# Block steps of a four-layer sequence kernel: the gated squares in quarters, their halves added on GpSimd, one matmul a group

## The reference, cut to what matters

```python
zxbcdt = rmsnorm(x, norm_w) @ Win                  # 64 -> z 128, x 128, B 16, C 16, dt 8
xBC = silu(causal_conv(zxbcdt[..., 128:288], Wconv, bconv))
dt = softplus(zxbcdt[..., -8:] + dt_bias); A = -exp(A_log)
y = ssd(xh, dt, A, B, C) + rev(ssd(rev(xh), rev(dt), A, rev(B), rev(C)))
y = (y + D * xh) * silu(z)                         # 128 inner channels, the "gated" y
y = y * rsqrt(mean(y * y, -1) + 1e-6) * gn_w       # the mean over the 128 channels of a token
x = x + y @ Wout
```

## Time and profile before

| what | value |
|---|---|
| median of three runs | 2499.17 us |
| span of the profiled execution, first to last instruction | 2496.4 us |
| PE busy | 1980.1 us, 79% |
| DVE busy | 1670.7 us, 67% |
| ACT busy | 1666.6 us, 67% |
| POOL busy | 1090.7 us, 44% |
| mean granted TensorE clock | 0.891 |

### The profile page before, as it was taken

The page is one execution under the profiler, slowest core; times in us unless marked ns, Lnnn a source line. Parts: engine busy times, 40 slices in busy tenths (PEclk is TensorE's granted clock), DMA queues, the critical chain, the costliest instruction groups (busy, mean ns, idle before and its releaser), DMA issues.

```text
span 2496.4 us, 58563 instructions
## 1 busy us (share of the span) xinstructions
PE 1980.1 (79%) x24262; PEld 1001.1 (40%) x24262; DVE 1670.7 (67%) x2423; ACT 1666.6 (67%) x2731; POOL 1090.7 (44%) x858
## 2 busy tenths in 40 slices
PE   4367677776777679979979979967997997996996
PEld 3122222222222235535525535534553552553553
DVE  3488888888888766556656656656655765665663
ACT  1276677676676657757857857866775775785784
POOL 0044444444444525516606625623551660662563
PEclk6578888888988889989989989988988998998997
DMA  4000000000000021022012111102102201211111
GB/s 159 0 0 1 1 0 0 1 1 0 1 1 0 0 65 38 18 65 49 19 56 47 30 55 39 39 18 62 41 14 66 49 18 56 47 30 42 40 39 35
DMA packets 95513, 77.46 MB, mean 31 GB/s; under 512 B 65936, under 2 KB 74128, under 8 KB 94736
## 3 DMA queue, kind: packets, MB, share of 16 engines
q1 hardware_dynamic: 91984, 73.32, 11.7%
q10 hardware_dynamic: 3264, 0.39, 0.1%
HBM read 27.02 MB, written 11.53 MB: 15 GB/s over the span
## 4 chain that ended last, share of the span: by engine, by line
PE 55%; DVE 20%; ACT 15%; issue 6%; POOL 2%; DMA 1%; ACTq 0%; POOLq 0%; SPq 0%; DVEq 0%
PE bank L593 10%; PE bank L662 7%; PE bank L625 6%; PE bank L674 6%; PE bank L606 5%; PE bank L682 5%; DVE Z L1271 4%; PE bank L521 3%; ACT bank L935 3%; PE bank L577 2%; ACT Z L827 2%; DVE XP L1337 2%; ACT SS L832 2%; DVE bank L1263 2%; POOL Y L986 2%
## 5 line engine op out<-in xcount | busy, mean ns | idle before, releaser
L986 POOL TENSOR_TENSOR Y<-Z 128x512 f32<-128x512 f32 x256 | 330.6, 1292 | 496.9 <-DVE Z L1271 320.4
L1018 POOL TENSOR_TENSOR SQ<-SQ,folded_weights 128x512 f32<-128x512 f32 x192 | 243.8, 1272 | 676.0 <-DVE SQ L1448 675.9
L1271 DVE TENSOR_TENSOR_SCAN Z<-SS,bank 128x512 f32<-128x512 f32 x256 | 309.9, 1211 | 0.5
L521 PE MATMUL bank<-Y,constants 128*128 128x512 f32 x512 | 298.0, 668 | 7.7 <-DVE bank L1279 7.6
L1024 POOL TENSOR_TENSOR SQ<-O,SQ 128x512 f32<-128x512 f32 x208 | 264.8, 1274 | 64.9 <-ACT O L931 36.5
L593 PE MATMUL bank<-folded_weights,work 128*64 128x128 f32 x4096 | 287.2, 285 | 0.0
L625 PE MATMUL bank<-SS,work 32*128 32x512 bf16 x1024 | 209.7, 389 | 63.0 <-ACT bank L935 45.0
L662 PE MATMUL bank<-SQ,work 128*32 128x64 f32 x8192 | 259.1, 227 | 0.6
L593 PEld LDWEIGHTS bank<-folded_weights,work 128*64 128x64 f32 x4096 | 225.9, 140 | 79.0 <-issue 79.0
L509 PE MATMUL bank<-work,Z 96*128 96x512 bf16 x256 | 113.8, 445 | 175.1 <-DVE Z L1271 175.0
L1390 DVE SCALAR_TENSOR_TENSOR work<-SQ,bank 64x512 f32<-64x512 f32 x256 | 175.5, 685 | 108.7 <-ACT SQ L903 106.6
(11 more groups left out here) (264 smaller groups left out, 3757.5 us busy)
## 6 DMA issues: line engine op xcount, KB each, us to landing
work<-XP SPq DMA_DIRECT2D x256, 134.0 KB, 2.4
decays_kept<-extra SPq DMA_DIRECT2D x24, 384.0 KB, 2.3
SS<-decays_kept SPq DMA_DIRECT2D x256, 24.0 KB
block_weights<-callw SPq DMA_DIRECT2D x8, 735.0 KB, 4.3
work<-decays_kept SPq DMA_DIRECT2D x240, 24.0 KB
Z<-state_sel SPq DMA_DIRECT2D x1, 2048.0 KB, 13.2
out<-O SPq DMA_DIRECT2D x2, 1024.0 KB, 8.5
constants<-consts SPq DMA_DIRECT2D x1, 1451.5 KB, 6.3
```

The lines of the kernel that those rows point to most:

```text
L521: mm(bank[7], ident, hc[ta % 4], start=(ta % S1 == 0), stop=(ta % S1 == S1 - 1), skip_group_check=True).then_inc(sg("s1_acc"), 1)
L986: g.tensor_tensor(hc[t_ % 4], hs[t_ % 4], c_copy[t_ % 4], ALU.mult).then_inc(sg("s1_hc"), 1)
L1018: g.tensor_tensor(MM[u % 3], MM[u % 3], Dhalf, ALU.add).then_inc(sg("mixed"), 1)
L1271: v.tensor_tensor_scan(hs[t_ % 4], decay1[t_ % 2], bank[B_BANKS[t_ % 3]], 0.0, ALU.mult, ALU.add).then_inc(sg("s1_h"), 1)
```

## The change

ScalarE squares 256 columns of both halves at a time: the quarter k = 2g in slot 9 + 8g (slot 1 of the period) and the quarter k = 2g + 1 in slot 13 + 8g (slot 5), the last one in slot 65 as before. GpSimd adds the two halves of the quarter in place, 128x256, before its work for u = 11 + 4k; the adds 14 and 15 come after the loop, ahead of grow(6). TensorE waits for both adds of the group and does one float32 matmul in the place of two.

```diff
+        def squares_of(k):
+            return O[:, 0:1024].rearrange("p (h n) -> p h n", h=2)[:, :, 256 * (k % 2):256 * (k % 2) + 256]
@@ TensorE
                 def sum_squares(g):
-                    pe.wait_ge(sg("gated_squared"), c * 8 + g + 1)
+                    pe.wait_ge(sg("squares_added"), c * 16 + 2 * g + 2)
...
-                    for hd in range(2):
-                        last = mm(bank[sum_bank(g)], C("ssum"), squares[hd], start=(hd == 0), stop=(hd == 1))
-                    last.then_inc(sg("squares_psum"), 1)
+                    mm(bank[sum_bank(g)], C("ssum"), squares[0], start=True, stop=True).then_inc(sg("squares_psum"), 1)
@@ ScalarE
-                    g = every(tau, 8, 13, NGROUP, ((7, L + 1),))
-                    if g is not None:
-                        act.wait_ge(sg("gated"), c * 16 + 2 * g + 2)
-                        if g >= 1:
-                            act.wait_ge(sg("squares_psum"), c * 8 + g)
-                        for hd in range(2):
-                            last = A(squares[hd], Z2[:, TOK * hd + BANK * g:TOK * hd + BANK * g + BANK], ACT.Square)
-                        last.then_inc(sg("gated_squared"), 1)
+                    for half, offset, moved in ((0, 9, ()), (1, 13, ((7, L + 1),))):
+                        g = every(tau, 8, offset, NGROUP, moved)
+                        if g is not None:
+                            k = 2 * g + half
+                            act.wait_ge(sg("gated"), c * 16 + k + 1)
+                            if g >= 1:
+                                act.wait_ge(sg("squares_psum"), c * 8 + g)
+                            A(squares_of(k), Z2.rearrange("p (h n) -> p h n", h=2)[:, :, 256 * k:256 * k + 256],
+                              ACT.Square).then_inc(sg("gated_squared"), 1)
@@ GpSimd
+                def add_squares(k):
+                    pool.wait_ge(sg("gated_squared"), c * 16 + k + 1)
+                    part = squares_of(k)
+                    g.tensor_tensor(part[:, 0, :], part[:, 0, :], part[:, 1, :], ALU.add).then_inc(
+                        sg("squares_added"), 1)
+
                 for u in range(L):
+                    if u >= 11 and (u - 11) % 4 == 0:
+                        add_squares((u - 11) // 4)
                     if u >= 20 and (u - 20) % 8 == 0:
                         grow((u - 20) // 8)
...
+                add_squares(14)
+                add_squares(15)
                 grow(6)
                 grow(7)
```

## The result

The changed kernel takes 2468.51 us (median of four runs, 2464.49 to 2471.06) against 2498.68 us for the kernel before in the same comparison; the ratio is 0.9873, 95% interval 0.9856 to 0.9891.

The account below looks back on a forecast made before the run. TensorE was taken to bound most of each period, waiting for ScalarE in slots 4 and 5. Span 2496.4 - 45.8 (loop matmuls) - 0 (block ends) = 2450.6 us, plus 2.8 to the median: 2453 us, range 2430 to 2482.

Parts of the forecast that it names:

- 45.8 us of span: Forecast saving: 0.955 us for each of 48 groups in the loop, with nothing for the block ends.
- One matmul of two goes: TensorE's sum of squares in the loop: two of four instructions leave, saving 0.955 us a group.
- What an add costs: One 128x256 add on GpSimd was taken as 0.69 us, from the memsets' fixed part and a 128x512 add.
- both covers in the loop: Odd add done 0.26 us before TensorE's sum; even add makes a product 0.2 us late, hidden by TensorE's wait for ScalarE.
- The end of a block: I take 0: From slot 58: adds lose 2.2 us, matmuls gain 1.7 and 0.96, low clock takes 0.5 to 1; net 0 a block.
- the bounds: Limits for the net effect at a block's end: 2.7 us gained to 2 us lost.
- I add nothing: In the loop, where the granted clock is low and the matmul costs more, no extra saving was counted.
- a rival for all periods together: Clock falls in every loop period, losing 1.13 us each, 54 us in all; 2523 us, chance 0.07.
- Its own sign: Prediction wrong if windows at clock 0.50 exceed those at block starts and ends and one a block in the loop.
- free adds: Rival: adds at the block end cost nothing, both matmuls count whole, 21 us more gained; 2432 us, chance 0.20.
- the dear add: Rival: a GpSimd add takes 1.27 us, showing in each period and at block ends; 2485 us, chance 0.12.
- ScalarE as the bound: Rival: ScalarE bounds the whole period, so TensorE's shorter work only means more waiting; 2499 us, chance 0.05.

Follow-up runs that it names:

- e9: Changed kernel with TensorE doing the product of u = 4 mod 8 twice, filling its slot 5 wait; 2446.0 us, 0.9790 of the kernel before.
- e8: Kernel before with only the product of u = 4 mod 8 done twice, filling TensorE's slot 5 wait; 2474.6 us, ratio 0.9897.
- e1: Changed kernel without GpSimd's adds, one matmul a group, so summing half of the channels only; 2457.3 us, 0.9804 of the kernel before.
- e2: Changed kernel with its adds kept but the two matmuls a group of the kernel before; 2533.2 us, 1.0106 of the kernel before.
- e3: Kernel before with only ScalarE's squares in quarters (slots 1 and 5), no adds, two matmuls; 2500.0 us, ratio 0.9983.
- e7: Changed kernel, even add just ahead of odd, adds 12 to 15 behind the last mixing, product of u = 4 mod 8 done twice; 2437.4 us, 0.9747 of before.
- e5: Changed kernel with GpSimd's even add moved right ahead of the odd one, where its queue is idle; 2464.4 us, 0.9858 of the kernel before.

## Why the prediction was off by a third of the gain

The range held and the mechanism was right in the loop: the sum of a group lies in the stretch in which TensorE never waits, so a matmul less shortens the period; e9 against e8 shows it with the clock out of the way. The 45.8 us of span became 27.3 us by these steps.

**"One matmul of two goes: 1.91 / 2 = 0.955 us."** The period got 0.86 us shorter (18.65 to 17.79). Four instructions took 1.91 us, two take 1.05, not 0.955. The two rows give an estimate of 0.43 us an instruction and a fixed 0.2 us behind the last one before TensorE goes on (4 x 0.43 + 0.2, 2 x 0.43 + 0.2). 48 x 0.095 = 4.5 us too much. Halving a chain row halves its fixed part too, which the change does not.

**"What an add costs: 0.69 us."** 0.729 us, and both covers in the loop were right to 0.01 us and in kind (0.27 us ahead of the sum, 0.20 us late at the product).

**"The end of a block: I take 0."** From group 5 on the ends got 1.8 us shorter, of which group 5's own matmul is 8 x 0.86 = 6.9: so the ends proper lost 5.1 us, 0.6 a block. The size is inside the bounds. The loss was sized about right. Against e1, which has no adds, the ends of the changed kernel are 242.4 - 222.3 = 20.1 us longer, 2.5 a block: the sum of group 6 starts 2.1 us later, where 2.2 were worked out, and the projections take 0.4 longer ((37.1 - 33.8) / 8) at the low clock, where 0.5 to 1 were. (With two matmuls, e2, the adds cost 3.1.) What was sized wrong is the gain, 1.7 + 0.96 = 2.7 us a block for the matmuls of groups 6 and 7: e1 has 22.0 / 8 - 0.86 = 1.9, and 1.9 - 2.5 is the 0.6 lost. The matmul of group 6 that goes ran at the low clock, but the low clock does not end the sooner for it, so the projections behind move into it: 33.8 us for the eight blocks in e1, 29.1 before.

**"I add nothing" for the clock in the loop.** This was the step that failed most: a term put at nothing. In the loops before, 9 falls cost 757.6 - 40 x 18.64 = 12.0 us, 1.3 us each; in the changed kernel 13 falls cost 729.6 - 40 x 17.78 = 18.4 us, 1.4 us each. So 6.4 us of the gain went to the clock. I had this as a rival for all periods together and with a price of 1.13 us a fall; it came in part, and belonged into the sum and not beside it. Its own sign for this, more than one stretch at 0.50 a block in the loop, came true (13 in eight blocks), but could not have told anything, since the kernel before had 9 already. e1, with 18 falls, shows that the adds are not what brings them, and e2 and e3, whose periods are 18.64 us, have 10 and 11.

What the falls hang on is shown by e7, e8 and e9: with TensorE's wait in slot 5 filled there is none, at either length of the period. It is not the narrow products, since the filling is more of them. The place fits too: in the kernels without the filling all 101 falls begin 1.1 to 2.8 us ahead of a sum, so behind the wait of slot 5. Whether it is the wait itself or the little work around it no run tells apart, since the repeated product changes both.

That the low clock takes more of the changed kernel is no chance of one execution: its four runs have mean granted clocks of 0.880 to 0.883 and those of e1 0.879 to 0.884, the thirteen of before next to e1 0.885 to 0.894. That mean holds the whole span; how many falls the loops have is counted in one execution of each kernel, and why the shorter period has more of them with its waits no longer than before is not settled.

The Trainium skill, "TensorE: Matmul & The Clock Gate", section "A second HAM failure mode: psum-queue depth-cycling", says that short idle times between groups of matmuls can make the clock oscillate when they come often enough. The trace agrees, for another kind of kernel than the page's: TensorE waits 0.59 us once a period before, 0.20 and 0.32 us in the changed kernel, and the clock fell 9 and 13 times in 40 periods.

The three steps make 4.5 + 5.1 + 6.4 = 16.0 us of the 45.8 - 27.3 = 18.5; the other 2.5 us lie outside the loops and ends, most of them ahead of the first block's first sum (1.0) and behind the last block (1.2), and no run was made to explain them.

Of the rivals, free adds are out (e1 and e2), the dear add is out (0.729 us), and ScalarE as the bound is out (e3, and a period that did shrink).

## What to carry to other kernels

A resource with room on average is full somewhere: GpSimd at 44% took 128 adds for nothing in the loop and cost 2.5 us at each block's end, where its queue had some 0.35 us of slack. Read the queue in every stage the new work lands in, and put the work where the queue waits anyway (e5, by its profile). Where the clock is low, do not count a saving at its full length: what follows can move into the low clock in its place, as the projections did in e1. And where TensorE waits for a few tenths of a microsecond once a period, look at the granted clock before and after: here filling the wait with repeated work gave 1.0% on the kernel before, nearly as much as the change itself.

## What was not expected of the hardware

Filling one wait a period gave the kernel before 24 us of span back, its loops and ends being 757.6 + 244.3 us and those of the same kernel with one product repeated in each period 745.8 + 231.9. No page total showed what there was to gain: the mean granted clock rose only from 0.891 to 0.905. The repeated products themselves cost nothing: the period with them stays at 18.64 us.
